# A graph layer's early gathers on one core: two low-half transfers, four node-row loads and a store of staged edges change places

## The reference

```
edge_index = stack([src, dst])
x = x + gnn(layernorm(x), edge_index)   # h = x @ W; deg and 1/sqrt(deg) per node;
                                        # out[dst] += h[src] * dinv[src] * dinv[dst]; + b; prelu
x = x + ffn(layernorm(x))               # one routing decision for all tokens (mean over nodes),
                                        # top 2 of 8 experts, gelu, layernorm, gamma and beta
```

## Time and profile before

| | |
|---|---|
| runs | 1012.9, 1022.06, 1023.15 us |
| profiled execution | 1009.26 us |
| its span | 1007.8 us |
| TensorE busy | 977.4 us (97%) |
| VectorE busy | 846.2 us (84%) |
| GpSimd busy | 553.6 us (55%), nearly all of it before 664 us |
| ScalarE busy | 504.6 us (50%) |

### The profile page before, as it was taken

One profiled execution on the slowest core, in us unless ns is written; L12 is line 12 of the kernel. 1 busy time (PEld: TensorE's weight loads), 2 busy tenths in 40 slices (PEclk: granted clock), 3 DMA queues, 4 the chain that ended last, 5 costly groups with the idle time before them and its releaser, 6 DMA issues.

```text
span 1007.8 us, 20238 instructions
## 1 busy us (share of the span) xinstructions
PE 977.4 (97%) x6920; PEld 829.0 (82%) x6921; DVE 846.2 (84%) x1741; ACT 504.6 (50%) x998; POOL 553.6 (55%) x511
## 2 busy tenths in 40 slices
PE   8899979999999999999999999999999999999996
PEld 7787767888888888888888887887889999999996
DVE  6988958889989999898999987995787878778886
ACT  6595533444444444444444444443856556464741
POOL 4067868787887887888788887741011110111111
PEclk9999998999999999999999999999999999999999
DMA  9059995766666577566675766756211111111101
GB/s 309 14 165 206 213 220 142 170 160 161 158 152 165 143 166 175 138 173 170 149 173 136 179 153 162 178 133 204 71 39 51 37 52 42 52 42 47 47 21 37
DMA packets 73697, 131.09 MB, mean 130 GB/s; under 512 B 10660, under 2 KB 54446, under 8 KB 73614
## 3 DMA queue, kind: packets, MB, share of 16 engines
q0 software_dynamic: 32448, 90.88, 38.7%
q1 hardware_dynamic: 41166, 39.12, 12.2%
HBM read 70.48 MB, written 28.03 MB: 98 GB/s over the span
## 4 chain that ended last, share of the span: by engine, by line
PE 37%; POOL 32%; DMA 13%; issue 10%; DVE 4%; ACT 2%; SPq 0%; ACTq 0%; DVEq 0%; POOLq 0%
POOL fetched L843 19%; PE banks L2151 12%; DMA partial<-fetched 9%; PE banks L2165 9%; PE banks L2040 6%; PE banks L2170 4%; POOL partial L843 4%; POOL partial L856 3%; PE banks L1877 3%; POOL extra_src L798 2%; POOL extra_row L811 2%; DMA fetched<-h_rows,node_row 1%; POOL staging L781 1%; PE banks L2016 1%; DMA partial<-h_rows,node_row 1%
## 5 line engine op out<-in xcount | busy, mean ns | idle before, releaser
L2040 PE MATMUL banks<-tab,adj 128*128 128x512 f32 x2009 | 502.0, 399 | 1.3 <-ACT adj L1759 1.3
L2040 PEld LDWEIGHTS banks<-tab,adj 128*128 128x128 f32 x2009 | 366.7, 189 | 72.9 <-DVE tab L1158 1.5
L1754 ACT CAST adj<-banks 128x784 fp32r<-128x784 f32 x320 | 244.7, 817 | 330.8 <-PE banks L2016 330.7
L843 POOL DMA_INDIRECT fetched<-h_rows,node_row x240 | 305.3, 1272 | 82.9 <-issue 65.3
L1041 DVE TENSOR_TENSOR hot_src<-iota_src,turned 128x2048 bf16<-128x2048 bf16 x164 | 199.9, 1219 | 36.4 <-PE banks L2016 36.0
L2016 PEld LDWEIGHTS banks<-hot_key,hot_src 128*128 128x128 bf16 x2560 | 124.3, 98 | 50.9 <-issue 30.9
L1041 DVE TENSOR_TENSOR hot_key<-iota_key,turned 128x1568 bf16<-128x1568 bf16 x164 | 158.7, 968 | 0.0
L2016 PE MATMUL banks<-hot_key,hot_src 128*128 128x98 bf16 x2560 | 148.2, 209 | 9.3 <-DVE hot_key L1041 8.6
L2165 PE MATMUL banks<-W2s,gh 128*128 128x512 f32 x384 | 137.4, 399 | 0.6 <-DVE pre L1572 0.6
L1805 ACT ACTIVATE gh<-banks,b1e 128x384 fp32r<-128x384 f32 (+1 forms) x136 | 79.8, 587 | 88.5 <-PE banks L2151 88.4
L2170 PE MATMUL banks<-W2s,gl 128*128 128x256 f32 x392 | 110.0, 281 | 0.0
(11 more groups left out here) (260 smaller groups left out, 1143.0 us busy)
## 6 DMA issues: line engine op xcount, KB each, us to landing
partial<-fetched POOLq DMA_DIRECT2D x48, 640.0 KB
xin<-in_x SPq DMA_DIRECT2D x49, 128.0 KB
x_dram<-x SPq DMA_DIRECT2D x49, 128.0 KB, 2.5
x1f<-x_dram POOLq DMA_DIRECT2D x16, 384.0 KB, 3.8
out<-res SPq DMA_DIRECT2D x48, 128.0 KB, 1.7
h_rows<-tab SPq DMA_DIRECT2D x5, 1024.0 KB, 7.5
h_rows<-tab POOLq DMA_DIRECT2D x5, 1024.0 KB, 12.7
W1a<-in_W POOLq DMA_DIRECT2D x8, 512.0 KB, 6.1
```

What stands on the lines that cost most here:

```text
L843: g.indirect_dma_start(out=into, out_offset=None, in_=h_rows, in_offset=bass.IndirectOffsetOnAxis(ap=node_row[:, m, r:r + 1], axis=0), bou ...
L1754: s.copy(adj[k][:, :].rearrange("p (q n) -> p q n", n=P)[:, :, at:at + 2 * BANK_NODES].rearrange("p q (b n) -> p q b n", b=2), bank_pairs[ ...
L2040: last = mm(acc[k][:, :], adj[k][:, q * P:(q + 1) * P], tab[:, q, :], start=(at == 0), stop=(at == T - 1), skip_group_check=True)
```

## The change

GpSimd: the last four of the eight node-row loads go from ahead of low parts 0 and 1 to behind staging batch 2. Of the extra sources only those of blocks 0 and 1 (4 DMAs) stay ahead of low part 2; low parts 2 to 5 follow one another; those of blocks 2 to 7 (12 DMAs) go behind staging batch 3. The number of DMAs is the same.

SyncE: batch 3 is stored in the loop, behind the stores and loads of block 1. The read-back of a pair of edges waits for its own batch, not for all three.

```
--- before.py
+++ after.py
@@ SyncE @@
                     if i == 2:
                         keep_staged(1)
-                keep_staged(2)
                 for d in range(T):
                     sp.wait_ge(epi, d * EPI + (2 * EPI + 5))
...
                     if q < NP:
-                        if q == DIRECT:
-                            sp.wait_ge(raw_kept, (NP - DIRECT) * 16)
+                        sp.wait_ge(raw_kept, ((q - DIRECT) // BATCHED + 1) * BATCHED * 16)
                         sp.wait_ge(raw_free, q + 1)
                         sp.dma_start(raw[:, q % 2, :, :].rearrange("r p s -> r (p s)"), staged[q]).then_inc(raw_back[q % 2], 16)
+                    if d == 1:
+                        keep_staged(2)
                     if d == GATHERED[-1]:
                         load_late()
@@ GpSimd @@
-                for m in range(NGATH):
+                for m in range(NGATH // 2):
                     load_node_src(m)
                 for i in range(2):
                     add_low_rows(i)
                 pool.wait_ge(raw_kept, 16 * BATCHED)
                 for q in STAGED[1]:
                     stage_edges(q)
+                for m in range(NGATH // 2, NGATH):
+                    load_node_src(m)
                 pool.wait_ge(extra_edge_made, CHUNKS)
-                for m in range(NGATH // 2):
+                for m in range(2):
                     load_extra_src(m)
-                for i in range(2, 4):
-                    add_low_rows(i)
-                for m in range(NGATH // 2, NGATH):
-                    load_extra_src(m)
-                for i in range(4, len(TABLE_PARTS)):
+                for i in range(2, len(TABLE_PARTS)):
                     add_low_rows(i)
                 pool.wait_ge(raw_kept, 32 * BATCHED)
                 for q in STAGED[2]:
                     stage_edges(q)
+                for m in range(2, NGATH):
+                    load_extra_src(m)
                 pool.wait_ge(h_summed, 16 * len(TABLE_PARTS))
```

## The result

| comparison | changed kernel, median us | kernel before, median us | ratio, 95% interval |
|---|---|---|---|
| first, 4 runs each | 1036.28 (1031.64 to 1041.13) | 1018.76 (1012.90 to 1023.15) | 1.0176 [1.0097, 1.0255] |
| second, 10 runs | 1018.58 (1012.32 to 1024.68) | 1009.38 | 1.0090 [1.0056, 1.0125] |
| third, 10 runs | 1025.04 (1014.99 to 1029.10) | 1016.31 | 1.0093 [1.0054, 1.0133] |

Predicted were 1031 us (1015 to 1038) and a shift of 9.0 us, which is 0.9%. The changed kernel is slower, and the first time lies in the range. The size of the shift was met where many runs were compared, and missed by 8.5 us in the first comparison (17.5 us between the medians).

What follows compares the result with a forecast made beforehand. GpSimd's gathers and TensorE's dense work, meeting at block 40, were taken as the bound. TensorE 5.2 later, plus 5.4 less 2.4 waiting, gave 8.2; 0.8 for clock made 9.0, on median 1022.06: 1031 us, range 1015 to 1038.

Steps and rivals of the forecast that it cites:

- Batch 3 off SyncE's path: At x for block 2: storing batch 3 behind block 1 removes TensorE's 8.3 us loss, alone worth nothing at the end.
- VectorE stands from 85 to 96, 11 us: At `node_rows(0)`: VectorE waits 11 us for the last node-row load, bounds 10.4 and 16.4.
- TensorE 11 us later and 2.5 more for half clock: At window 1: VectorE's wait and half clock delay TensorE 13.5 us, less 8.3, so 5.2 later from block 2 on.
- GpSimd 8.2 us later: At GpSimd's first gather: new load order moves it from 137.67 to 145.6; stream 8.2 us later, bounds 1.9 and 11.8.
- The sums land 8.2 us later at block 40: At block 40: gathered sums land at 618.9 instead of 610.7; VectorE waits 8.1 us, TensorE loses 5.4 instead of 2.4.
- the 0.8 us: At the block 40 pause: half clock may return for 0 to 2.5 us; 0.8 was taken.
- The end moves with GpSimd alone: At block 40: while VectorE's wait for gathers exceeds 2.7 us, only GpSimd's lateness moves the end.
- 2.7 us: At block 40: VectorE's wait of 5.1 less TensorE's loss of 2.4, the delay VectorE can take before TensorE feels it.
- GpSimd catches up: Rival, GpSimd's loads before the gathers: steps of 1.31 us make it 1.9 late; end +3, 1025 us; chance 0.15.
- Faster: Rival: node-row wait hidden, GpSimd fills its gaps; -4.3 us, 1018 us; needs gathers starting before 137.67; chance 0.08.

Runs made afterwards that it cites:

- sync_only: The kernel before with only SyncE's part of the change, batch 3 stored behind block 1; 1010.75 us, ratio 1.0005 to the kernel before.
- after_again: The changed kernel run again without any edit, for a second trace; median 1018.58 us, ratio 1.0090 to the kernel before.
- wait_only: `sync_only` with VectorE's first `node_rows` also waiting for staging batch 2, GpSimd's order as before; 1016.41 us, ratio 1.0027 to the kernel before.
- before_again: The kernel before run again unchanged, as a control; 1018.53 us, ratio 1.0044 to itself.
- pool_only: The changed kernel with SyncE's part undone, so GpSimd's new order alone; 1025.07 us, ratio 1.0109 to the kernel before.
- own_sem: The changed kernel with the last four node-row loads on a semaphore of their own; 1013.69 us, ratio 1.0032 to the kernel before; repeated on another chip, 1.0036.
- gather_late: `sync_only` plus eight unread single-word indirect loads ahead of GpSimd's first gather; 1023.81 us, ratio 1.0135 to the kernel before.
- best: `sync_only` with the four extra-source loads of blocks 6 and 7 moved behind staging batch 3; 1016.63 us, ratio 0.9993 to the kernel before.
- nodes_first: The changed kernel with all eight node-row loads back ahead of low parts 0 and 1; 1016.69 us, ratio 1.0067 to the kernel before.

## Why the prediction was right, and where it was not

- **Batch 3 off SyncE's path: 8.3 us free, worth 0.** Shown by `sync_only`, to within 3 us.
- **VectorE stands from 85 to 96, 11 us.** It stood until 95.12, 10.08 us. The last node-row load started at 92.63 and had landed 2.5 us later (2.8 assumed). In the other three traces of the changed order the wait was 6.5 to 8.5 us, since VectorE came later.
- **TensorE 11 us later and 2.5 more for half clock.** Its count matmuls of window 1 went from 89.07 to 99.28, 10.2 later; x1 of block 1 from 123.59 to 135.41, 11.8 later, so the clock took 1.6. The Trainium skill (TensorE: Matmul & The Clock Gate, "HAM oscillation — how this bites in real kernels") has the slower clock come back at each such pause; the trace agrees, 0.50 at 98 to 100 us. By block 35 TensorE was 3.4 us behind, not 5.2.
- **GpSimd 8.2 us later.** 9.63 us of idle time ahead of low part 0 (9.0 predicted), low part 4 at 111.10 (111.77), the wait for low halves gone. The 18 loads behind the low parts took 114.73 to 144.00 with their gaps, 29.3 us (30.0). First gather 144.00 instead of 145.6: 6.3 us later. (The prediction's own figures give 7.9 + 0.2 = 8.1, and 115.6 + 18 x 1.31 = 139.2 for the lower bound, where it has 8.2 and 139.5; neither slip matters.)
- **The sums land 8.2 us later at block 40.** 3.5 in `after_again`. The gather stream, taken as fixed, is not: from the first gather to the last sum of block 40 it took 473.0 us before, 470.1 here, and 469.0 to 474.9 in the other six of the eight executions above (481.6 in `wait_only`). These 6 us of spread are as large as the effect. VectorE's wait was 5.16 us and TensorE lost the same 2.4: no half clock, the 0.8 us were not paid there.
- **"The end moves with GpSimd alone."** This step failed. The sum was made on an execution in which the gathers had 2.7 us over TensorE, and carried to a median 12.8 us longer, as if those 12.8 us lay beside the meeting. The table shows where they can lie: in pauses of TensorE ahead of it. Where those are longer than the slack, TensorE sets the end and the node-row wait adds to it; SyncE's 8.3 us are not gained either, because x then lands in time anyway (`before_again` and `pool_only` have no wait at line 1211 without the edit). This weighing of two kinds of execution is how we read one profile per kernel; no run isolates it, and on the chip of `own_sem`, where the node-row wait cost 0.58%, no profile shows an execution of the second kind. Averaged over executions, the node-row wait costs 0.45 to 0.6%, where it was put at 0, and GpSimd's order the rest, 0.3 to 0.45%, where it was put at all 9 us. The total, 0.9%, agreed because one was too small by about what the other was too large. That is luck, and not the mechanism of the sum.
- **The first comparison's other 8.5 us.** No rival had them. In its profile they are pauses that end by nothing shown; the control shows that the kernel before has such pauses, not that they are equally long there. `pool_only` and `gather_late`, on a second chip, had medians 1.1 and 1.35% up. Whether a late node-row wait makes a long pause more likely stays open: two comparisons of 10 runs at 1.009 speak against it, four runs at 1.0176 do not exclude it. The cause of the pauses is open too.
- The rivals: "GpSimd catches up" (1025 us) was the nearest to the execution of `after_again`, +3.5 against its +3, though by the gather stream and not by shorter loads. "Faster" and its condition, a gather before 137.67, are out: no changed order had one, not even `best`, which was made for it.

## What to carry to other kernels

When two streams meet with a slack of 2.7 us and the runs spread by 10, there is no single bound: price each edit against both streams and weigh them by how often each one sets the end; the difference between the profiled time and the median says that the profile may show only one of the two cases. A counting semaphore over eight loads makes the first use wait for the last load: moving any of them moves the wait, and a semaphore of its own for the late half takes back more than half of this change's loss. Issuing transfers earlier need not start what depends on them earlier: in `best` GpSimd stood 8.05 us further on.

## What the runs showed of the hardware

- **Pauses without a releaser.** In the four traces of one chip (`after_again`, `sync_only`, `nodes_first`, `own_sem`), and in that of the earlier trace rows, TensorE's waits between 60 and 200 us, less those for node rows and x, are 2.7 to 3.3 us; in the seven traces of two other chips 6.7 to 15.9, and in the first comparison's 25. The kernel before has a median of 1009.38 us on the first of these chips and 1016.59 and 1016.31 on the others. ScalarE's waits marked "remote", over the whole span, say the same: there are none in the first five traces and 7 to 32 us in the other eight. So the pauses go with the chip or the hour more than with the kernel; no run tells those two apart, nor shows that the 7 us between the medians are the pauses.
- **GpSimd can be held between two indirect loads**, 8.05 us in `best`, while the DMA engines' share is over 1.1; at a share of 1.24 shortly before it was not.
- **The prologue comes in two lengths, with TensorE's granted clock.** Over 36 to 56 us the mean granted clock is 0.66 or 0.67 in the six executions with a late low part 0 and 0.83 to 1.00 in the seven others, at 18.7 to 20.0 us busy in all of them. `own_sem` had 0.66 in one execution and 1.00 in the other. Why the clock stayed low there is open.
